# Transformer block with routed experts: GpSimd's queue reordered, scores bank by bank, Q/K and layer-norm work moved to other steps

## What is computed

```python
xn = layernorm(x)
# attention: 16 heads of 16, blocks of W = 64 queries against 3 blocks of keys, |i - j| <= 64
a  = softmax(mask(q @ k.T * scale)) @ v @ Wo + bo      # q, k, v = xn @ W + b
h  = layer_norm(a + xn, g1, b1)
m  = layer_norm(gelu(h @ W1 + c1) @ W2 + c2 + h, g2, b2)
# routed experts: each token goes to one of 8 experts, a 256 x 256 matrix
chosen = argmax(xn @ gate_w.T)
e  = xn + expert_w[chosen] @ xn
out = x + m + e
```

## Time and profile before

| | |
|---|---|
| three runs | 1461.51, 1473.32, 1473.76 us (median 1473.32) |
| profiled execution | 1471.13 us, its span 1469.3 us |
| mean granted TensorE clock | 0.928 |
| TensorE matmuls busy | 1200.0 us |
| VectorE busy | 924.3 us |
| GpSimd busy | 825.5 us |
| ScalarE busy | 726.5 us |

### The profile page before, as it was taken

The page is one execution under the profiler, slowest core; times in us unless marked ns, Lnnn a source line. Parts: engine busy times, 40 slices in busy tenths (PEclk is TensorE's granted clock), DMA queues, the critical chain, the costliest instruction groups (busy, mean ns, idle before and its releaser), DMA issues.

```text
span 1469.3 us, 32444 instructions
## 1 busy us (share of the span) xinstructions
PE 1200.0 (82%) x11720; PEld 726.1 (49%) x11720; DVE 924.3 (63%) x2207; ACT 726.5 (49%) x1355; POOL 825.5 (56%) x1088
## 2 busy tenths in 40 slices
PE   0717898799879898898987898798986989878877
PEld 0414454554637445464545546374454645365445
DVE  8554657476656746776575766577474765656455
ACT  1304657146562574436572575526763365725661
POOL 6551568435781567625674457815676266834664
PEclk9958999899989899999998999898998999999989
DMA  8443081231723254230812327231532408122010
GB/s 250 120 130 116 31 199 50 80 127 44 163 76 104 73 132 99 72 125 31 199 51 80 126 59 156 69 109 67 147 85 72 124 32 202 54 85 87 3 29 29
DMA packets 93977, 142.89 MB, mean 97 GB/s; under 512 B 10592, under 2 KB 62688, under 8 KB 91744
## 3 DMA queue, kind: packets, MB, share of 16 engines
q1 hardware_dynamic: 87680, 124.04, 30.6%
q0 software_dynamic: 6144, 16.79, 3.6%
HBM read 74.47 MB, written 68.29 MB: 97 GB/s over the span
## 4 chain that ended last, share of the span: by engine, by line
PE 42%; POOL 26%; issue 12%; DVE 7%; ACT 3%; DMA 3%; another core or an unknown queue 0%; DVEq 0%; POOLq 0%; SPq 0%; ACTq 0%
PE bank L1180 6%; PE bank L1268 5%; PE bank L1078 5%; PE bank L1081 5%; PE bank L1079 5%; PE bank L1173 4%; POOL x_sb L521 4%; DVE m_sb L745 4%; POOL xs_dram L507 4%; POOL res_r L527 3%; POOL pool L496 3%; POOL pool L499 3%; POOL x_sb L483 3%; POOL x_sb L480 3%; PE bank L1148 2%
## 5 line engine op out<-in xcount | busy, mean ns | idle before, releaser
L981 ACT ACTIVATE pool<-bank 128x512 f32<-128x512 f32 x512 | 285.5, 596 | 150.9 <-PE bank L1180 147.5
L745 DVE TENSOR_REDUCE m_sb<-bank 128x2 f32<-128x384 f32 x512 | 261.5, 552 | 130.3 <-PE bank L1188 128.7
L468 POOL TENSOR_SCALAR_AFFINE_SELECT pool<-pool 128x512 f32<-128x512 f32 x256 | 183.6, 717 | 244.1 <-ACT pool L981 205.5
L1180 PE MATMUL bank<-q_s,k_s 128*128 128x256 f16 x1024 | 185.1, 289 | 15.7 <-ACT pool L981 8.8
L412 POOL TENSOR_TENSOR rs<-ve,neghalf 128x1 f32<-128x1 f32 x64 | 36.9, 577 | 251.7 <-DVE ve L806 251.7
L1268 PE MATMUL bank<-pool,v_a 128*32 128x256 f32 (+2 forms) x2560 | 166.7, 352 | 8.4 <-POOL pool L473 8.3
L970 ACT ACTIVATE xn<-bank 128x256 f32<-128x256 f32 x120 | 46.0, 384 | 224.4 <-PE bank L1081 218.6
L1173 PE MATMUL bank<-k_s,q_s 48*64 48x192 f16 x2048 | 99.1, 270 | 58.9 <-DVE m_sb L745 40.5
L1180 PEld LDWEIGHTS bank<-q_s,k_s 128*128 128x128 f16 x1024 | 82.5, 101 | 126.3 <-issue 97.4
L820 DVE TENSOR_TENSOR pool<-pool 128x512 f16<-128x512 f32 x128 | 105.5, 827 | 62.1 <-ACT pool L995 52.7
L473 POOL TENSOR_SCALAR_AFFINE_SELECT pool<-pool 128x512 f32<-128x512 f32 x208 | 133.4, 641 | 0.0
(11 more groups left out here) (154 smaller groups left out, 2644.6 us busy)
## 6 DMA issues: line engine op xcount, KB each, us to landing
pair_dram<-pool SPq DMA_DIRECT2D x96, 256.0 KB, 4.2
xn<-xs_dram SPq DMA_DIRECT2D x40, 384.0 KB, 3.6
ys_dram<-xn SPq DMA_DIRECT2D x120, 128.0 KB, 1.8
q_s<-pair_dram SPq DMA_DIRECT2D x32, 384.0 KB, 6.7
k_s<-pair_dram SPq DMA_DIRECT2D x32, 384.0 KB, 8.3
x_sb<-in_L_attn_x SPq DMA_DIRECT2D x8, 1024.0 KB, 5.8
res_dram<-x_sb SPq DMA_DIRECT2D x8, 1024.0 KB, 5.2
res_r<-res_dram SPq DMA_DIRECT2D x8, 1024.0 KB, 5.0
```

The costliest lines, as they stand in the source:

```text
L468: nc.gpsimd.affine_select(out=p, in_=p, compare_op=ALU.is_ge, fill=0.0, base=0, pattern=[[0, 4], [1, 2 * W]], channel_multiplier=-1).then_ ...
L745: nc.vector.tensor_reduce(m_sb[:, 4 * g + par:4 * g + 4:2, t], SB[par][:, 0:2 * WIN].rearrange("p (h c) -> p h c", h=2), AX.X, ALU.max).th ...
L981: nc.scalar.activation(prob[:, (k + 2) % 3, par::2, :], TB[par][:, :].rearrange("p (h q) -> p h q", h=2), ACT.Exp, scale=EXP_SCALE).then_i ...
L1180: return nc.tensor.matmul(out[:, i * QW:i * QW + QW], k_s[:, h, W + t * P:W + t * P + P], q_s[:, 2 * h + par, t * P:t * P + QW], start=Tru ...
```

## The change

1. SP: `store_res(b + 1)` ahead of `stack_loads` 2, 3; `load_x` of the next-but-one input after expert store 2, not 10.
2. GpSimd: the 16 adds of `residual` become one per step in steps 6 to 21; the gathers of `fetch` come first after the masks, its adds (`add_fetched`) stay behind `residual_attn`; `rstd` of the input's statistics moves from step 8 to the start of the turn.
3. VectorE: the input statistics of b + 2 go into the W2 stage (two tiles in each of W2 tiles 4 to 7, `c1_stage` behind them), for input 1 into the prologue. `xn` in steps 2 to 5 (was 10 to 13), its transposes in 6 to 9 (was 14 to 17).
4. The 24 thirds of Q and K are spread over steps 12 to 31: one or two a step (was two in 18 to 29).
5. TensorE: in the attention steps scores are issued bank by bank, each bank behind one `scores_t`, each waiting for its own maximum. The scores in the W1 and W2 stages stay as they were.
6. Transposed maxima get banks of `XB` (MB0, MB1, MB0, SB1) and wait only for their own group's maxima; the scores no longer wait for them, but the transposes of `xn` and the first third do.

```diff
-    XN_AT = T + 2
+    XN_AT = 2
     XT_AT = XN_AT + 4
-    QK_AT = XT_AT + 4
+    QK_AT = T + MAX_AT
+    RES_AT = XN_AT + 4
+    def thirds_at(k):
+        n = STEPS - QK_AT
+        return range(max(0, k - QK_AT) * 24 // n, max(0, k + 1 - QK_AT) * 24 // n) if k < STEPS else range(0)
+        XB = [MB[0], MB[1], MB[0], SB[1]]
# SP
-                    if i == 10 and x_next:
+                    if i == 2 and x_next:
                         load_x(b + 1)
...
+                    store_res(b + 1)
                     for i in range(2, 4):
                         stack_loads(b + 1, i)
-                    store_res(b + 1)
# GpSimd
+            def residual_tile(b, i):
+                t = i % T
+                if i == 0:
+                    pool.wait_ge(xn_rdy.sem, xn_rdy.at(b, T))
+                if i < T:
+                    nc.gpsimd.tensor_tensor(x_sb[:, t, :], x_sb[:, t, :], xn[:, t, :], ALU.add).then_inc(res_p.sem, 1)
+                else:
+                    pool.wait_ge(res_p.sem, res_p.at(b, t + 1))
+                    nc.gpsimd.tensor_tensor(x_sb[:, t, :], x_sb[:, t, :], bc[:, 3, :], ALU.add).then_inc(res_p.sem, 1)
             def turn(b, last):
+                if not last:
+                    rstd(b + 1, 0, ve0, rs0)
                 for k in range(STEPS):
                     band(b, k)
-                    if k == T and not last:
-                        rstd(b + 1, 0, ve0, rs0)
-                if not last:
-                    residual(b + 1)
+                    if RES_AT <= k < RES_AT + 2 * T and not last:
+                        residual_tile(b + 1, k - RES_AT)
+                fetch(b, last)
                 rstd(b, 1, ve1, rs1)
                 if not last:
                     residual_attn(b + 1)
-                fetch(b, last)
+                add_fetched(b)
# VectorE, W2 stage
                     f_out(b, t)
+                    if t >= TH and b < NB - 2:
+                        for i in range(2 * (t - TH), 2 * (t - TH) + 2):
+                            c1_tile(b + 2, i)
                 if not last:
                     keep_positions(b + 1)
+                if b < NB - 2:
+                    c1_stage(b + 2)
# TensorE
+            def scores_half(b, j, par):
+                scores_wait(b, j, par)
+                for i in range(2):
+                    for n in range(2):
+                        score_mm(SB[par], n, j, par, i)
+                for n in range(2):
+                    mm = mask_mm(SB[par], n, j % T, par)
+                mm.then_inc(S_ps.sem, 1)
-            def max_cols(b, g, issued):
-                pe.wait_ge(mx.sem, mx.at(b, 2 * issued))
-                nc.tensor.transpose(SB[g % 2][0:4 * T, 0:P], ...
+            def max_cols(b, g):
+                pe.wait_ge(mx.sem, mx.at(b, 2 * T * (g + 1)))
+                if g == 2 and b < NB - 1:
+                    pe.wait_ge(xT_l.sem, xT_l.at(b + 1, 3))
+                nc.tensor.transpose(XB[g][0:4 * T, 0:P], ...
                     for par in range(2):
                         if k < STEPS:
                             scores_t(b, k, par)
-                        if QK_AT <= k < QK_AT + 12 and not last:
-                            qk_third(b + 1, *divmod(2 * (k - QK_AT) + par, 3))
-                    if 1 <= k and k - 1 + LEAD < STEPS:
-                        scores(b, k - 1 + LEAD)
+                        if not last:
+                            for third in list(thirds_at(k))[par:par + 1]:
+                                qk_third(b + 1, *divmod(third, 3))
+                        if 1 <= k and k - 1 + LEAD < STEPS:
+                            scores_half(b, k - 1 + LEAD, 1 - par)
```

More of the change, by code:

```diff
@@ L91, in build @@
     assert len(W1_STEPS) + T == LEAD
-    MAX_STEPS = [LEAD - T + 3] + [T * g + MAX_AT - 1 + LEAD for g in range(G - 2)]
+    def thirds_at(k):
+        n = STEPS - QK_AT
+        return range(max(0, k - QK_AT) * 24 // n, max(0, k + 1 - QK_AT) * 24 // n) if k < STEPS else range(0)
     def tiles_at(t):
@@ L859, in turn @@
                         maxima(b, k - 1 + LEAD)
-                    if k < T and not last:
-                        c1_tile(b + 1, k)
-                    if k == T and not last:
-                        c1_stage(b + 1)
                     if k in SHARED:
@@ L870, in turn @@
                         xn_low(b + 1, k - XT_AT)
-                    if QK_AT <= k < QK_AT + 12 and not last:
-                        for third in range(2 * (k - QK_AT), 2 * (k - QK_AT) + 2):
+                    if not last:
+                        for third in thirds_at(k):
                             if third % 3 == 2:
@@ L914, in _ @@
                 maxima(0, LEAD - T + t)
+            for t in range(T):
+                c1_tile(1, t)
+            c1_stage(1)
             assert done == N_PREP, done
@@ L1091, in xn_transposes @@
                 pe.wait_ge(xn_rdy.sem, xn_rdy.at(b, TH * (u // DC) + TH))
+                if u == 1 and not first:
+                    pe.wait_ge(mT_ev.sem, mT_ev.at(b - 1, 2))
                 if u >= 2:
@@ L1106, in qk_third @@
                         pe.wait_ge(xT_l.sem, xT_l.at(b, 4))
+                    if u == 0 and b:
+                        pe.wait_ge(mT_ev.sem, mT_ev.at(b - 1, 3))
                 if part < 2:
@@ L1203, in scores_wait @@
                     pe.sem_inc(passed, 1)
-                if j in MAX_STEPS and par == 1:
-                    pe.wait_ge(mT_ev.sem, mT_ev.at(b, MAX_STEPS.index(j) + 1))
-                    pe.sem_inc(passed, 1)
             def scores(b, j, first=False):
@@ L1401, in _ @@
                 if t == 3:
-                    max_cols(0, 0, LEAD - T + t)
+                    max_cols(0, 0)
                 scores(0, LEAD - T + t, first=True)
```

20 lines of the change are left out of this document (9 added, 11 removed).

## The result

The kernel after takes 1589.7 us (median of four runs, 1577.3 to 1602.1) against 1473.5 us (1461.5 to 1474.7): a ratio of 1.077, 95% interval 1.068 to 1.086. The forecast was 1433 us, so it had the wrong sign. The profiled execution has a span of 1585.1 us, at a mean granted clock of 0.853 where before had 0.928.

The account below looks back on a forecast made before the run. Between W1 and W2 the GpSimd queue was taken as the bound. A turn gains 7 us, less W2's 1.5: -5.5, six -33; odd turn -2, last -4, prologue +1: -38 from 1471.1 to 1433 us, range 1420 to 1448.

Parts of the forecast that it names:

- Scores bank by bank: Attention steps on TensorE: issuing each bank's scores separately costs 0.74 us a step instead of 0.49, but removes the maxima wait.
- The clock is half there anyhow: Turn start: the granted clock is already half at 655 to 665 us; 1.3 us was taken for the later start.
- the sign turn at about +0.35: Attention steps: an added cost of about +0.35 us a step would turn the forecast gain into a loss.
- Rival C: Attention scores: column halves sharing rows do not overlap, +0.73 us a step in 18 steps, 1516 us; chance 0.07.
- it would be wrong if score steps took over 2.4 us: Attention steps: a sign against the forecast, pointing to Rival C; steps 22 to 30 were expected near 1.7 us.
- Attention -1.1: Step 5 to the last mask: 54.2 us after the change against 55.3 before, so 1.1 us less a turn.
- Fetch 7.2 us behind the last mask: GpSimd's gathers start once the residual's store has landed, at 727.5 instead of 743.4 us.
- `rstd` late, W1 2.6 us later: The first layer norm's `rstd` stands behind the gathers, ending at 740.3 against 737.73 us; W1 ends 2.6 us late.
- `send` done 43 us behind the last mask: GpSimd's scatters end at 763.6 us instead of 773.66; rows are back by 768.4, before TensorE asks.
- `residual_mlp` 15 us beside W1: GpSimd's MLP residual, 11.5 us with VectorE idle, takes 15 overlapping W1; first expert about 779 against 785.94, 7 us won.
- B: Rival: W1 becomes the bound through late `rstd`, half clock and blocked VectorE; a turn gains 0 to 3, 1455 us; chance 0.20.
- W2 +1.5 and the turn's start +1.3: Statistics lengthen three W2 tiles by 0.7 us, net +1.5; `c1_stage` and `rstd` ahead of the first mask cost 1.3.

Follow-up runs that it names:

- joined: The kernel after, with the attention steps' scores of both banks issued together again as in before: 1429.9 us, ratio to before 0.970.
- heads alternating: The kernel after, with scores still in two alternating slices, but cut by head, each for both banks: 1472.9 us, ratio to before 1.001.

## Why the prediction was wrong, step by step

*Scores bank by bank.* This step failed, in two terms.

The first is the clock, which the sum put at nothing. It priced the order at full clock and kept for after the half clock of ten microseconds ("The clock is half there anyhow"). Measured are 27 to 58 us of it in seven of eight turns, and an attention 12.7 us longer where -1.1 was forecast. What was missing is that the matmuls in a stretch decide how soon the clock returns in it. The plain steps of the last turn took 3.2 to 3.6 us, where I had "perhaps 0.1" gained for each.

The second is the price at full clock. The sum has 0.74 us a step instead of 0.49, so +0.25. But the rows beside it give 0.17 + 0.23 = 0.40 for the joined order, and one bank after the other takes 0.80: +0.40, and +0.42 over steps 6 to 18 of the first turn. The forecast itself let the sign turn at about +0.35. So the change would have won next to nothing even with before's clock: heads alternating, which pays most of this price (30.6 us for those steps, where joined takes 26.5) and keeps the clock, came out at 1.001 of before.

*Rival C* ended near (1516) and on the right side by the wrong mechanism: it priced column halves that do not overlap. They do: four 192-column matmuls of a bank take 146.03 - 145.84 = 0.19 us. Of C only the sentence "it would be wrong if score steps took over 2.4 us" held. The forecast had no rival in which the half clock lasts longer, though the earlier trace rows showed the clock falling behind pauses.

The Trainium skill (TensorE: Matmul & The Clock Gate, Part 1) says that the clock follows how busy TensorE has been. Taken as time in use the traces disagree: 10.00 of 10.00 us busy at 0.50. The runs differ in how much of the array worked at a time, and none shows what the chip itself counts.

*The rest.* With the scores joined, the remaining edits give 1429.9 us, where the whole was forecast at 1433: per turn -5.4 us against my -5.5. That is chance, for two reasons. The joined kernel does not pay the +0.25 a step that stood in the forecast's attention, and the terms differ:

- *Attention -1.1:* measured -6.5, of which 2.8 only moved ahead of the first mask.
- *Fetch 7.2 us behind the last mask:* 9.3. GpSimd and SP of after:

```profile
776.80 1.05 POOL L534 DMA_INDIRECT x_sb<-ys_dram,pos_y  x1 [9.33 <-DMA res_dram<-x_sb]
```
```profile
759.14 10.83 SPq L288 DMA_DIRECT2D pair_dram<-pool  x6
770.02 0.60 SPq L313 DMA_DIRECT2D res_dram<-x_sb  x1
```

  The store went out 2.6 us behind the mask (forecast 1.8) and landed 0.8 slower than put.
- *`rstd` late, W1 2.6 us later:* 4.6. TensorE waited 5.25 us instead of 4.4 for n1, and around the end of that wait the granted clock was 0.59 and 0.56 in two windows of 4 us (788 to 796). Taking the power between the gathers gave back 4.1.
- *`send` done 43 us behind the last mask:* 47. A wait that I had not seen stands ahead of it, 5.08 us for the positions, which come late because W1 starts late:

```profile
804.37 1.05 POOL L520 DMA_INDIRECT xs_dram<-xn,pos  x1 [5.08 <-DVE pos L736]
```
- *`residual_mlp` 15 us beside W1:* 12.7. But it does hold W1, as the earlier trace rows warned and B priced. VectorE's two subtractions take 6.21 us instead of 0.69 each, and TensorE stands 4.15 us behind them:

```profile
814.64 5.48 POOL L509 TENSOR_TENSOR pool<-pool,bc 128x256 f32<-128x256 f32 x8
```
```profile
815.60 6.21 DVE L836 TENSOR_TENSOR pool<-pool 128x512 f16<-128x512 f32 x2 [0.18 <-ACT pool L1015]
```
```profile
822.89 0.54 PE L1197 MATMUL bank<-k_s,q_s 48*64 48x192 f16 x8 [4.15 <-DVE m_sb L761]
```

  W1 takes about 30 us in five of seven turns instead of 24.4. The passage from the last mask to the first expert gained 2.3 us, not 7: B's mechanism, in the size that B gave it.
- *W2 +1.5 and the turn's start +1.3:* together +3.3 up to the first mask; the last three tiles grew by 0.5 each. TensorE's wait for the first masked probabilities is 0.26 us in the turn read above and 0.8 to 1.2 in others, so most of the turn's start cost nothing.

## What to carry to other kernels

An order that cuts small, packed matmuls into thinner slices is to be priced at both clocks, with the question what would bring the full clock back. Here TensorE was busy all the time at 0.50, and what helped was not more time in use but the same matmuls four corners at a time, or full-size ones beside them. When a wait moves instead of going away, look at what the waiting instruction itself needs: here one wait for sixteen sums stood ahead of work that needed none of them. A block of GpSimd sums beside VectorE's work with two SBUF inputs is to be counted as one instruction of the block's length, here up to 5 us.

## What the runs showed of the hardware that I had not expected

The granted clock stayed at 0.50 for 50 us in which TensorE was busy nearly without a gap, with 64-row matmuls that use one row half at a time between full-size ones. With the same matmuls on both row halves it was back within ten microseconds, and within 14, where it fell at all, with 15 full-size ones of 512 columns added in five steps.

Two neighbouring groups of score matmuls on different row halves ran at the same time (eight took 0.19 us from their start to the masks'), and one after the other when 128 x 128 matmuls stood between them (0.19 for four, then again).

VectorE was shut out for what was left of a block of GpSimd's sums: 5.14 us for an instruction that takes 0.22 in before, while a single sum takes 0.69. With a wait behind each sum the same comparison took 0.59 at most. The Trainium skill (SBUF — State Buffer, Who interferes with whom) has the holder keep the shared ports for one instruction; here GpSimd kept VectorE out over nearly all of a block of eight.
